# Every second down product as three short-form passes: a sandwich block of attention and mixture of experts on one core

## The reference

```python
topk_idx, topk_w = _router(x, gate_w, e_bias)          # 6 of 32 experts per token, in 4 of 8 groups
combine = zeros((T, 32)).at[arange(T)[:, None], topk_idx].add(topk_w)
h = relu2(einsum('th,eih->tei', x, up_w))              # 32 experts x 64 hidden units
h = h * combine[:, :, None]
moe_out = einsum('tei,ehi->th', h, down_w)
shared = relu2(x @ shared_up_w.T) @ shared_down_w.T    # 256 hidden units
return moe_out + shared
```

## Time and profile before

| | |
|---|---|
| runs shown | 563.09 us median of 3 (561.16 to 565.19) |
| the profiled execution's own time | 559.93 us |
| its span | 558.1 us |
| PE busy, share of the span | 510.7 us, 92% |
| DVE busy | 401.1 us, 72% |
| ACT busy | 370.2 us, 66% |
| POOL busy | 154.2 us, 28% |
| mean granted clock of TensorE | 0.993 |

### The profile page before, as it was taken

How to read it: one execution, slowest core, us unless ns; L and a number is a source line. 1 busy time by engine, 2 the same in 40 slices (tenths; PEclk the granted TensorE clock), 3 DMA queues, 4 the chain that set the end, 5 groups by cost and what they waited for, 6 DMA issues and landing times.

```text
span 558.1 us, 10016 instructions
## 1 busy us (share of the span) xinstructions
PE 510.7 (92%) x3120; PEld 303.4 (54%) x3120; DVE 401.1 (72%) x1076; ACT 370.2 (66%) x758; POOL 154.2 (28%) x448
## 2 busy tenths in 40 slices
PE   2379999899999999999798999999999999999993
PEld 1225555466555556656344666565666666666661
DVE  6677677688888787778692687767685959576453
ACT  2308678677888887787866657676666675755442
POOL 5142121114234414122011230525243351312010
PEclk9999899999999999999999999999999999999998
DMA  6333372333333233333101526535454453635421
GB/s 175 105 116 100 113 250 68 113 104 116 105 98 107 68 102 103 116 102 102 58 3 51 187 93 177 180 97 168 145 171 156 133 193 94 195 106 192 154 80 38
DMA packets 52260, 67.41 MB, mean 121 GB/s; under 512 B 5168, under 2 KB 36528, under 8 KB 51952
## 3 DMA queue, kind: packets, MB, share of 16 engines
q1 hardware_dynamic: 52208, 66.78, 38.1%
HBM read 51.17 MB, written 15.20 MB: 119 GB/s over the span
## 4 chain that ended last, share of the span: by engine, by line
PE 66%; SPq 11%; DMA 8%; ACT 6%; DVE 5%; issue 3%; POOL 0%; ACTq 0%; DVEq 0%
PE pY L1206 11%; PE pS L1206 11%; PE pO L1128 6%; PE pS L1192 6%; PE pS L1194 6%; PE pS L1193 6%; PE pS L1116 5%; PE pS L1105 5%; SPq L381 5%; DMA k_scratch<-k_parts 4%; SPq L369 4%; DMA kp<-k_scratch 4%; ACT probs L602 3%; SPq L389 2%; DVE mneg L819 2%
## 5 line engine op out<-in xcount | busy, mean ns | idle before, releaser
L819 DVE TENSOR_REDUCE mneg<-pS 128x2 f32<-128x512 f32 x256 | 163.8, 686 | 38.0 <-PE pS L1105 36.2
L602 ACT ACTIVATE probs<-pS 128x512 f32<-128x512 f32 x256 | 140.5, 599 | 44.9 <-PE pS L1116 44.3
L677 ACT ACTIVATE h_ring<-r 128x512 f32<-128x512 f32 x144 | 90.4, 630 | 88.5 <-DVE r L973 68.4
L973 DVE SCALAR_TENSOR_TENSOR r<-pS,c_ring 128x512 f32<-128x512 f32 x128 | 87.6, 689 | 45.8 <-PE pS L1194 44.2
L1105 PE MATMUL pS<-kp,qp 96*128 96x256 bf16 x512 | 102.5, 285 | 11.4 <-DMA kp<-k_scratch 10.6
L1116 PE MATMUL pS<-qp,kp 102*128 102x512 bf16 x256 | 98.5, 387 | 6.9 <-ACT probs L602 5.2
L1192 PE MATMUL pS<-qp,up_hi 128*128 128x512 f32 x144 | 103.5, 719 | 0.7 <-ACT probs L602 0.7
L1105 PEld LDWEIGHTS pS<-kp,qp 96*128 96x128 bf16 x512 | 44.9, 100 | 57.6 <-DMA kp<-k_scratch 16.0
L1206 PE MATMUL pS<-h_ring,down_sb 128*128 128x512 f32 x144 | 73.8, 594 | 0.0
L1206 PE MATMUL pY<-h_ring,down_sb 128*128 128x512 f32 x144 | 73.4, 595 | 0.0
L1128 PE MATMUL pO<-probs,vv 128*32 128x256 f32 x1024 | 69.5, 389 | 0.0
(11 more groups left out here) (177 smaller groups left out, 668.5 us busy)
## 6 DMA issues: line engine op xcount, KB each, us to landing
c_ring<-c_scratch SPq DMA_DIRECT2D x64, 512.0 KB, 4.0
qp<-q_scratch SPq DMA_DIRECT2D x64, 96.0 KB
kp<-k_scratch SPq DMA_DIRECT2D x64, 96.0 KB
q_scratch<-q_parts SPq DMA_DIRECT2D x16, 192.0 KB, 2.0
k_scratch<-k_parts SPq DMA_DIRECT2D x16, 192.0 KB, 2.1
q_scratch<-q_parts SPq DMA_DIRECT2D x16, 128.0 KB, 2.0
k_scratch<-k_parts SPq DMA_DIRECT2D x16, 128.0 KB, 1.9
out_x<-ot SPq DMA_DIRECT2D x7, 256.0 KB, 4.5
```

Source lines behind the costliest of these rows:

```text
L602: nc.scalar.activation(probs[j][:, sh], pS2[n % S2_RING][:, :, :], ACT.Exp, scale=SCALE).then_inc(exp_done, 1)
L677: nc.scalar.activation(h_sb[n % HRING], r_sb[n % URING][:, :], ACT.Square).then_inc(sq_done, 1)
L819: nc.vector.tensor_reduce(mneg[u % 2][:, :, hh, k], pS1[n % S1_RING][:, :].rearrange("p (a s) -> p a s", a=TH), AX.X, ALU.max, negate=True ...
L973: nc.vector.scalar_tensor_tensor(out=r_sb[n % URING][:, :], in0=pU[n % URING], scalar=0.0, in1=c_ring[group % CRING][:, at], op0=ALU.max, ...
```

## The change

Every odd block's down product is no longer one float32 product but three passes of split parts, like the up product: `down_hi` by `h_hi`, `down_lo` by `h_hi`, `down_hi` by `h_lo`. For this:

- GpSimd splits the odd blocks of the down weights in the attention phase, in three portions (`split_down`, behind units 19, 21 and 23).
- ScalarE squares r twice for an odd block: once into `h_hi` (float32r), once into h as before.
- VectorE subtracts: `low(n)` makes `h_lo` = h - `h_hi`. It is issued behind `rect(n + 2)`, ahead of the routing step of that block.
- `LAG` is 4 instead of 3, the h ring has 5 buffers instead of 4. `h_hi` and `h_lo` have two buffers each.
- Two of the four `c_ring` buffers, the fifth h buffer and the two output buffers now lie in the attention's probability tiles; SyncE waits for the last attention product before it loads into these two (`if n in (2, 3)`).

```diff
-HRING = URING = 4
+HRING, URING = 5, 4
+NSPLIT = FBLK // 2
...
-LAG = 3
+DOWN_AT = (19, 21, 23)
+LAG = 4
...
+                if n in (2, 3):
+                    sp.wait_ge(pv_done, 4 * NB)
...
+            def split_down(c):
+                part = slice(NSPLIT // 3 * c, NSPLIT // 3 * (c + 1))
+                pool.wait_ge(wb_loaded, 16 * N_WB)
+                nc.gpsimd.tensor_copy(down_hi[:, part], down_odd[:, part]).then_inc(dhi_done, 1)
+                pool.wait_ge(dhi_done, c + 1)
+                nc.gpsimd.tensor_tensor(down_lo[:, part], down_odd[:, part], down_hi[:, part].bitcast(F32),
+                                        ALU.subtract).then_inc(dlo_done, 1)
...
+                if u in DOWN_AT:
+                    split_down(DOWN_AT.index(u))
...
                 if n >= HRING:
                     act.wait_ge(down_done, n - HRING + 1)
+                if n % 2:
+                    if n >= 4:
+                        act.wait_ge(down_done, n - 3)
+                    if n == 1:
+                        act.wait_ge(pv_done, 4 * NB)
+                    nc.scalar.activation(h_hi[n // 2 % 2], r_sb[n % URING][:, :], ACT.Square).then_inc(hi_done, 1)
                 nc.scalar.activation(h_sb[n % HRING], r_sb[n % URING][:, :], ACT.Square).then_inc(sq_done, 1)
...
+            def low(n):
+                dve.wait_ge(hi_done, n // 2 + 1)
+                dve.wait_ge(sq_done, n + 1)
+                if n >= 4:
+                    dve.wait_ge(down_done, n - 3)
...
+                nc.vector.tensor_tensor(h_lo[n // 2 % 2], h_sb[n % HRING], h_hi[n // 2 % 2].bitcast(F32),
+                                        ALU.subtract).then_inc(lo_done, 1)
...
                 for k in range(FBLK):
                     rect(i, k)
+                    if (FBLK * i + k) % 2 and FBLK * i + k >= 3:
+                        low(FBLK * i + k - 2)
...
-                mm(pF[i % 2], down_sb[:, block], h_sb[n % HRING], start=k == 0,
+                if n % 2 == 0:
+                    mm(pF[i % 2], down_sb[:, block], h_sb[n % HRING], start=k == 0, stop=False).then_inc(down_done, 1)
+                    return
+                if n == 1:
+                    pe.wait_ge(dlo_done, 3)
+                pe.wait_ge(lo_done, n // 2 + 1)
+                mm(pF[i % 2], down_hi[:, block // 2], h_hi[n // 2 % 2], start=False, stop=False)
+                mm(pF[i % 2], down_lo[:, block // 2], h_hi[n // 2 % 2], start=False, stop=False)
+                mm(pF[i % 2], down_hi[:, block // 2], h_lo[n // 2 % 2], start=False,
                    stop=k == FBLK - 1).then_inc(down_done, 1)
```

More of the change, by code:

```diff
@@ L185, in block_kernel @@
         cT = sb("cT", [E, TILE])
-        c_ring = [sb(f"c_ring{i}", [P, CGROUP, TILE]) for i in range(CRING)]
+        c_ring = ([sb(f"c_ring{i}", [P, CGROUP, TILE]) for i in range(2)]
+                  + [probs[i][:, :, :, :].rearrange("p a b c -> p (a b c)").rearrange("p (k t) -> p k t", k=CGROUP)
+                     for i in (4, 5)])
         r_sb = [sb(f"r{i}", [P, TILE]) for i in range(URING)]
-        h_ring = sb("h_ring", [P, HRING, TILE])
-        h_sb = [h_ring[:, i] for i in range(HRING)]
+        down_hi, down_lo = sb("down_hi", [P, NSPLIT, D], F32R), sb("down_lo", [P, NSPLIT, D], F32R)
+        down_odd = down_sb[:, :, :].rearrange("p (a b) d -> p a b d", b=2)[:, :, 1]
+        h_ring = sb("h_ring", [P, HRING - 1, TILE])
+        spare = [probs[i][:, :, :, :].rearrange("p a b c -> p (a b c)") for i in range(3)]
+        h_sb = [h_ring[:, i] for i in range(HRING - 1)] + [spare[2][:, 0:TILE]]
+        h_hi, h_lo = ([sb(f"{name}{i}", [P, TILE], F32R)[:, :] for i in range(2)] for name in ("h_hi", "h_lo"))
         fT_sb = sb("fT_sb", [P, TILE])
-        assert HRING * TILE == RBLK * P and TILE >= SI
+        assert (HRING - 1) * TILE == RBLK * P and TILE >= SI
         up_in = [h_ring[:, i] for i in range(NCUT - 1)] + [fT_sb[:, 0:SI]]
@@ L195, in block_kernel @@
         fn = sb("fn", [P, C4, D])
-        ot = [sb(f"ot{i}", [P, C4, D]) for i in range(2)]
+        ot = [probs[3][:, :, :, :].rearrange("p a b c -> p (a b c)")[:, TILE * i:TILE * (i + 1)]
+              .rearrange("p (c d) -> p c d", c=C4) for i in range(2)]
         pS1 = [ps(f"pS1_{i}", [P, TILE]) for i in range(S1_RING)]
@@ L280, in block_kernel @@
         sq_done = sem("sq_done")
+        hi_done = sem("hi_done")
+        lo_done = sem("lo_done")
+        dhi_done = sem("dhi_done")
+        dlo_done = sem("dlo_done")
         down_done = sem("down_done")
@@ L965, in rect @@
                     dve.wait_ge(sq_done, n - URING + 1)
+                    if n % 2:
+                        dve.wait_ge(hi_done, (n - URING) // 2 + 1)
                 if k < SBLK:
@@ L975, in rect @@
                                                op1=ALU.mult).then_inc(rect_done, 1)
+            def low(n):
[4 more added lines that the diff above has]
+                if n == 1:
+                    dve.wait_ge(pv_done, 4 * NB)
+                nc.vector.tensor_tensor(h_lo[n // 2 % 2], h_sb[n % HRING], h_hi[n // 2 % 2].bitcast(F32),
+                                        ALU.subtract).then_inc(lo_done, 1)
             link = Link(dve, ln1_link, 0)
@@ L1061, in _ @@
                         stats_f(i - 1)
+            low(FBLK * NTILE - 1)
             stats_f(NTILE - 1)
```

## The result

The changed kernel takes 583.47 us in the median, against 562.48 for the kernel before: ratio 1.0366, 95% interval 1.0311 to 1.042. It is slower by 21 us, inside the range of 565 to 587 and 7.5 us above the forecast of 576. The profiled execution has a span of 581.3 us, 23.2 more than before.

What follows compares the result with a forecast made beforehand. TensorE was taken to bound the feed-forward phase; VectorE's late subtractions would stall it. Tile terms (stalls less savings) of +11.6 us plus 1.7 for the clock gave +13.3 on 563.1: about 576 us, range 565 to 587.

Steps and rivals of the forecast that it cites:

- Saving: Odd down products on TensorE: three short passes, 0.70 us instead of 0.86; 0.16 per odd block, 11.4 us in all.
- Place and size of the wait: TensorE waits for low(5) behind VectorE's backlog: 3.6 us a tile, part of it already on blocks 17, 1 and 3.
- the working: Tile 4 timelines from 427.44 us: TensorE reaches down block 5 at 442.1, low(5) ends at 445.7; stall 3.6 us.
- Held by GpSimd: VectorE instructions with two SBUF inputs wait for a running GpSimd one; the power holding low(5) costs 0.45 us a tile.
- The clock: TensorE's clock falls behind one of seven new feed-forward gaps: +1.7 us, bounds 0 and 12.
- attention: GpSimd's split of the down weights fits its idle time at no cost; otherwise up to 2 us three times.
- tile 0: low(7), behind the rect of block 9, is last and late: 3.1 - 1.4 = +1.7 us.
- the end: Tile 7 and the tail: nothing is late there, so only the saving remains, -1.4 us.
- case (d): Same stall, but ScalarE delays the exp 0.5 to 1 us a tile or most gaps drop the clock: 583 to 594; chance 0.25.
- (c): The predicted stall of TensorE behind VectorE's late subtraction, at the predicted size: 569 to 583 us; chance 0.52.
- VectorE keeps up behind block 5: After block 5 VectorE's work per two blocks fits against TensorE's 2.96 us, and it has caught up before block 17.
- rival (a): TensorE still bounds the feed-forward phase, so the gain of 11.4 us comes whole: 552 us; chance 0.08.

Runs made afterwards that it cites:

- layout alone: The changed kernel with every down product plain float32, one square and no subtraction, keeping layout, rings, LAG 4 and the weight split; 559.63 us, ratio 0.9976.
- the gap filled: The changed kernel with six extra passes of down_hi by h_hi before the wait for block 5's h_lo in tiles 1 to 6; 574.8 us, ratio 1.0243.
- the table of four: Tile times of LAG 4 and LAG 6, each with the router as changed (32.33, 32.07 us) and its steps two blocks later (31.25, 30.24 us).
- the kernel with late blocks: The changed kernel with short form only in odd blocks 9 to 15 (tile 0: 11 to 15; tile 7: all nine); 556.93 us, ratio 0.9924.
- seven of nine blocks: The changed kernel with LAG 6, router two blocks later, short form omitted in blocks 13 and 15 of tiles 1 to 6, three in tile 0; 560.65 us, ratio 0.9981.
- the later router with LAG 4: The changed kernel, LAG 4 kept, with the router's steps two blocks later in tiles 1 to 6; 573.02 us, ratio 1.0195.

## Why the prediction was right, and where it was not

**Saving: right.** 0.16 us per odd block forecast. Between the layout alone and the kernel without subtraction a tile goes from 30.18 to 28.67 us, 0.17 per odd block.

**Place and size of the wait: right.** The waits fell on the blocks named, 0.35 and 0.22 and then 2.12. `low(5)` started 17.26 us behind the tile's first rect; the working had 17.1 free and 17.6 held. Tile 1 took 32.33 us, forecast 32.4; tile 6 grew by 1.1, forecast 1.3.

**Held by GpSimd: half right.** The addition held VectorE as said, now `comb` (1.36 us, `root_c` behind it 0.28). But `low(5)` at 460.32 was not held by the power that ran from 459.85 to 460.87. Nor was any of the 72: the longest took 0.69. (The working has a slip of its own there: a subtraction held until 445.1 would end at 445.8, not 445.7.) The 0.45 a tile that I put on the hold are wrong, and that the stall came out is luck. From the down product behind up block 0 to the first pass of block 5 the working has 445.7 - 427.44 = 18.26 with the hold and 17.81 without; tile 4 took 461.15 - 442.86 = 18.29. In place of the hold stand three small amounts that the working left out: the first rect, now with the subtraction of block 15 in front of it, starts 0.20 behind that down product instead of 0.04; `low(5)` comes 0.2 later behind that rect than in the working without the hold; and 0.15 pass between its end and the first pass.

**The clock: mis-sized, the largest error.** I charged one fall in seven gaps, 1.7 us. The profiled execution has four, each of the 1.7 us forecast: 6.8. The chance was taken from gaps of attention; of the six gaps of 2.1 to 2.3 us in tiles 0 to 5, four were followed by a fall. The four tiles with a fall are of one length and repeat one pattern, so they are not four independent cases. In the profiled executions the difference is 23.2, 9.9 above the forecast of 13.3: 5.1 of it is the clock, 3.5 attention, 1.2 tile 0 and 0.6 the end, while the other tiles together, apart from the clock, took 0.5 less than forecast. By the medians the forecast was short by 7.7.

**Which case it was.** With 583.47 us and the clock falling behind most gaps, the result is at the foot of case (d), to which I gave 0.25, and not in (c), which had 0.52. The range held because it took in the lower part of (d).

**Tile 0: +2.9, forecast +1.7.** ScalarE's `keep_xT(1)` stands behind the second square of block 1, and TensorE waited 1.31 us for it instead of 0.80:

```profile
312.65 1.08 PE L1217 MATMUL pX<-gate_sb,xT 128*128 128x32 f32 x8 [1.31 <-ACT xT L586]
```

I had costed ScalarE at nothing there. The end was 0.8 shorter instead of 1.4.

**Attention: +3.5 us in the profiled execution, forecast 0.** The first rect came at 304.84 before, 308.34 changed, but at 304.99 with the layout alone, which has the same attention and the same split of weights, and at 304.4 with the gap filled. Over the profiled executions of all these kernels it lies between 304.4 and 309.1. The layout alone isn't slower than the kernel before either (0.9976), so the 3.5 us aren't the change's. Falls of the clock in attention differ between the executions and may be a part of it; what makes up the rest stays open.

**"VectorE keeps up behind block 5": wrong as a reason.** It kept up because TensorE had just stood still. I compared 28.1 us of VectorE work with 29.1 of TensorE, and left the wait for the exp out of the cycle. With it, by the rows of the kernel in which the subtraction isn't waited for: 28.3 + 2.3 = 30.6 even if ScalarE were on time (an estimate), and 32.1 as it was. So my picture of one wait that costs everything was incomplete. By that estimate rival (a) could not have come true even if `low(5)` had been early. Of rival (d) the exp delay by ScalarE is real too (2.34 to 3.45 us), though it shows only once the wait for `h_lo` is gone.

## What to carry to other kernels

Work put on an engine with idle time costs nothing only where that idle time is: count the engine's cycle with the waits that lie inside it, not its busy share, and look which engine ends those waits. When a named wait is removed and the time hardly moves, look for a second cycle of nearly the same length; vary two things, each with and without the other, as in the table of four, to tell them apart. A cheaper form that needs help from other engines can be used for just those blocks where they are free, as the kernel with late blocks does (ratio 0.9924, 0.9876 to 0.9972).

## What the runs showed of the hardware

- **The clock.** In the feed-forward phase gaps of 2.1 to 2.3 us in TensorE's dense work were followed by a stretch at 1.2 GHz, mostly of some 3.4 us, in seven cases out of ten: in four of six in the changed kernel and in three of four in tile 0 of other kernels (the subtraction left out, seven of nine blocks, the gap filled; not the later router with LAG 4). Gaps of 1.8 us were in two out of six. Eighteen gaps of 1.5 to 1.75 us in four kernels were followed by none, nor were those of 0.7 us in six tiles. 1.4 us of useless products in each of six gaps saved some 7 us.
- **GpSimd and VectorE.** A GpSimd addition of 128x512 held a VectorE instruction with two SBUF inputs for up to 1.1 us. The power of 128x4, 1.02 us long, did not hold a subtraction of 512 started 0.47 us into it; in eight cases of the changed kernel a subtraction started during such a power, and each took at most 0.69. The Trainium skill, "SBUF — State Buffer", section "Who interferes with whom", speaks of an exclusive lock on the ports that the two engines share, held for the whole instruction of the one that comes first; the addition agrees and the power does not. It may be that the power reads its few elements at the start and computes without the port; no run here shows that. The other way round, the power at 442.46 took 1.40 instead of 1.04 us, with a subtraction on VectorE from 442.28 on, and so in all four cases where the subtraction came first.
